# Slot order of the second attention, and identity transposes ahead of three long waits, in a two-layer attention and feed-forward kernel

## The reference, cut to what matters

```python
q, k = rmsnorm(q, q_norm_w), rmsnorm(k, k_norm_w)
scores = einsum('bkgqd,bksd->bkgqs', qg, k) / sqrt(HD)
attn = softmax(scores + where(rel > 0, NEG_INF, slopes * rel))
out = einsum('bkgqs,bksd->bkgqd', attn, v) ... @ Wo.T
w_up = (NF4[codes] * repeat(absmax, 64)).reshape(H, D).T
y2 = relu(x1 @ w_up + b_up + lora) @ w_down + b_down + lora
```

## Time and profile before

| | |
|---|---|
| runs | 1400.67, 1397.17, 1401.01 us; median 1400.67 |
| profiled execution | 1399.04 us; its span 1397.2 us |
| mean granted clock of PE | 0.992 |
| busy | PE 1342.4, DVE 933.1, ACT 880.2, POOL 661.8 us |
| HBM | 61.04 MB moved, mean 44 GB/s |

### The profile page before, as it was taken

One profiled execution on the slowest core, in us unless ns is written; L12 is line 12 of the kernel. 1 busy time (PEld: TensorE's weight loads), 2 busy tenths in 40 slices (PEclk: granted clock), 3 DMA queues, 4 the chain that ended last, 5 costly groups with the idle time before them and its releaser, 6 DMA issues. The chain is left out here.

```text
span 1397.2 us, 21472 instructions
## 1 busy us (share of the span) xinstructions
PE 1342.4 (96%) x7350; PEld 1075.9 (77%) x7350; DVE 933.1 (67%) x1659; ACT 880.2 (63%) x2167; POOL 661.8 (47%) x988
## 2 busy tenths in 40 slices
PE   6899889999999999999999999999999999999997
PEld 5543337888888888888888888888888887778886
DVE  5756655667776776767677767767676767676433
ACT  6246565777676776767777767767677766663211
POOL 5323256555455564535554544645355545443311
PEclk9989999999999999999999999999999999999999
DMA  4100032102010120202020101202020202024010
GB/s 164 53 1 1 0 106 72 31 1 62 26 52 11 52 77 1 62 11 67 2 61 27 52 11 52 72 6 62 3 75 1 62 11 50 9 92 129 27 61 31
DMA packets 36029, 61.04 MB, mean 44 GB/s; under 512 B 9200, under 2 KB 13424, under 8 KB 35920
## 3 DMA queue, kind: packets, MB, share of 16 engines
q1 hardware_dynamic: 35920, 59.66, 13.8%
HBM read 49.68 MB, written 9.96 MB: 43 GB/s over the span
## 5 line engine op out<-in xcount | busy, mean ns | idle before, releaser
L947 POOL TENSOR_TENSOR RI<-SM,C 128x1 f32<-128x1 f32 x256 | 152.2, 595 | 402.7 <-ACT PB L1310 402.4
L1791 DVE TENSOR_TENSOR R<-T,R 128x512 fp32r<-128x512 f32 x288 | 198.8, 691 | 115.2 <-ACT R L1383 104.7
L1784 DVE CUSTOM_DVE_ANT_0 PB<-S,REL,SLC 128x128 f32<-128x128 f32 (+7 forms) x256 | 204.6, 813 | 79.6 <-PE S L2039 76.5
L1310 ACT ACTIVATE PB<-PB,NM 128x128 f32<-128x128 f32 (+7 forms) x256 | 198.2, 774 | 44.7 <-DVE NM L1784 44.1
L1383 ACT ACTIVATE R<-T 128x512 fp32r<-128x512 f32 x288 | 171.4, 595 | 81.2 <-PE T L2428 78.2
L948 POOL TENSOR_SCALAR PB<-PB,RI 128x128 f32<-128x128 f32 (+7 forms) x256 | 209.9, 820 | 25.2
L2428 PE MATMUL T<-C,PB 128*128 128x128 f32 x1152 | 176.0, 276 | 7.7 <-DVE R L1791 3.3
L2428 PEld LDWEIGHTS T<-C,PB 128*128 128x128 f32 x1152 | 135.7, 141 | 37.8 <-DVE R L1791 13.6
L1370 ACT ACTIVATE DQ<-DQ 128x704 f32<-128x704 int32 x128 | 97.5, 785 | 78.6 <-DVE DQ L1865 76.4
L2037 PE MATMUL WB<-R,XT 128*128 128x512 f32 (+1 forms) x268 | 103.9, 388 | 0.0
L2039 PE MATMUL WB<-R,XT 128*128 128x512 f32 (+1 forms) x268 | 103.0, 384 | 0.0
(11 more groups left out here) (311 smaller groups left out, 3502.1 us busy)
## 6 DMA issues: line engine op xcount, KB each, us to landing
RAW<-w SPq DMA_DIRECT2D x85, 256.0 KB, 2.7
DQ<-codes SPq DMA_DIRECT2D x16, 352.0 KB, 4.0
DQ<-absmax SPq DMA_DIRECT2D x16, 352.0 KB, 2.8
dequantised<-DQ SPq DMA_DIRECT2D x16, 352.0 KB, 4.0
PB<-dequantised SPq DMA_DIRECT2D x5, 512.0 KB, 3.7
PB<-x SPq DMA_DIRECT2D x8, 256.0 KB, 4.0
PB<-x_scratch SPq DMA_DIRECT2D x8, 256.0 KB, 3.5
out<-PB SPq DMA_DIRECT2D x8, 256.0 KB, 2.0
```

Of the source, the lines that this page charges most:

```text
L947: ch.link(e.tensor_tensor(RI[:, k:k + 1], SM[:, k:k + 1], C[:, C_EXP + 5:C_EXP + 6], ALU.pow))
L1310: e.activation(pb(m, a, 0, L), pb(m, a, 0, L), ACT.Exp, scale=-1.0, bias=NM[:, k:k + 1], accum_out=SM[:, k:k + 1]).then_inc(exp_done, 1)
L1784: e.tensor_tensor_reduce(out=pb(m, a, 0, L), in0=bank[:, 0:L], in1=REL[:, TOK - L:TOK], scale=SLC[:, a:a + 1], scalar=3.0e38, op0=ALU.add, ...
L1791: e.tensor_tensor(r(o + 512, 512), bank[:, :], rf(o, 512), ALU.subtract).then_inc(t_free, 1)
```

## The change

In `slot_items`:

- `DB` no longer stands beside `DC`. It stays at the front in all slots with a further group and in even slots; in odd slots of the last group it goes behind the first exponential.
- `DC` in slots j = 1 with a further group goes from ahead of the first transpose (`T 0`) to behind it. In slot 57 it goes from the front to behind the last scores.
- `DD` in odd slots of the last group goes behind the third exponential.
- Chunks `W 0` and `W 1` of slot 57 go from between scores and first transpose to behind the first and the second exponential.
- In slot 61 the last exponential and its normalisation (`EX 3`, `NR 3`) go behind `FB 0`.
- `DA` in slots with j % 4 = 1 goes behind the transposes `T 4` to `T 7`; in slots with j % 4 = 3 it stays.

No item that PE takes part in changes its place among PE's own.

In PE's program `keep_warm(bank, n)` issues n transposes of the identity into one 128x128 corner of a bank, with no semaphore: 10 into S[0] ahead of the wait for the fourth Wqk product; 14 into the T bank in `turn_shift(0)`, ahead of the wait for the shifts; and 14 in slot 0's `QK`, behind the ring's wait and ahead of the wait for the scaled queries.

```diff
-    put("DC", "DB", when=0 < n < STEPS - 1 and not (j == 1 and kv))
+    put("DC", when=0 < n < STEPS - 1 and j != 1)
+    put("DB", when=0 < n < STEPS - 1 and (kv or j % 2 == 0))
     ffn(STEPS - 3, ("FB", 1))
     weights("W", 0, 1, when=kv)
     put("PQ", when=s2)
     head(0, "S")
     head(1, "S")
-    put("DC", "DB", when=j == 1 and kv)
     put("DU", when=j == 0)
-    weights("W", 0, 1, when=not kv)
     weights("Q", 0, 1)
     first = j in (1, 7) if kv else j % 2 == 1
     if first:
         keys(0)
+    put("DC", when=j == 1 and kv)
     head(0, "EX")
-    put("DD", when=j % 2 == 1 and n < STEPS - 1)
+    weights("W", 0, when=not kv)
+    put("DB", when=n < STEPS - 1 and not kv and j % 2 == 1)
+    put("DD", when=j % 2 == 1 and kv)
     put("PKV", when=kv)
...
         head(1, "EX", "NR")
+        weights("W", 1, when=not kv)
         head(3, "S")
+        put("DC", when=j == 1 and not kv)
         keys(2)
         ffn(STEPS - 1, ("FV", 1))
         weights("W", 2)
         head(2, "EX", "NR")
+        put("DD", when=not kv and n < STEPS - 1)
         keys(3)
         weights("W", 3)
         weights("Q", 2, 3)
-        head(3, "EX", "NR")
+        if n != STEPS - 3:
+            head(3, "EX", "NR")
         put("QN", when=s2)
         ffn(STEPS - 5, ("FA", 0))
-        ffn(STEPS - 3, ("FB", 0))
+        ffn(STEPS - 3, ("FB", 0), ("EX", 3), ("NR", 3))
         put("WO")
-        put("DA", when=n < STEPS - 1)
+        put("DA", when=n < STEPS - 1 and j % 4 == 3)
         ffn(STEPS - 5, ("FA", 1))
         keys(4, 5, 6, 7)
+        put("DA", when=n < STEPS - 1 and j % 4 == 1)
...
+            def keep_warm(bank, n):
+                for _ in range(n):
+                    e.transpose(bank[:, 0:P], IDENT, IDENT)
...
+            keep_warm(S[0], 10)
             pe.wait_ge(t_free, T_A["QK", 2, 1] + 1)
             qk(*QK_THEN[0])
...
                 mring(k)
+                if u == 0:
+                    keep_warm(T[k % 2], 14)
                 pe.wait_ge(shift_ready, u + 1)
...
                     elif it == "QK":
+                        if known == 0:
+                            ring(at(g, i, "QT"))
+                            keep_warm(T[AT[known, "QT"] % 2], 14)
                         pe.wait_ge(w_free, at(g, i, "PQ") + 1)
```

## The result

The changed kernel takes 1391.36 us in the median of six runs (1388.74 to 1395.60), the kernel before 1400.84 beside it (1396.86 to 1404.00); the ratio is 0.9939 with a 95% interval of 0.9921 to 0.9957. Run again later on another occasion, it gave 1392.48 (1389.79 to 1393.47) against 1400.03, ratio 0.9945 [0.9929, 0.9961]. So some 8 us are gained, against 9.2 forecast.

What follows compares the result with a forecast made beforehand. PE, busy 96% of the span, bounds the kernel; only gaps and low clock can give. 3.6 + 0 + 1.5 + 3.3 = 8.4 off 1399.04 gives 1390.6, said as median 1391.5 us; range 1386.5 to 1398.

Steps and rivals of the forecast that it cites:

- A: Identity transposes do not hold the clock, or the fall only moves elsewhere: median about 1395.5 us; chance 0.28.
- B: Time freed in the attention is met by the next wait and the clock gives little: 1398 us; chance 0.17.
- C: Slower: `DA`'s lines behind the last copies wait for codes or DMA and delay the next scores: 1405.5 us; chance 0.06.
- Part 1: Six slots j = 1 with a further group: `DC` behind the first low half gains 3.6 us, bounds 1.5 to 3.6.
- That is 0.6 each: Gain per slot j = 1 from moving `DC`: 0.44 us of PE idle and the refill behind it, six times.
- Part 2: `DA` behind the last transposes in slots j = 1 and 5: 0.8 of 2.3 us cover used, cost nothing.
- Part 3: Slot 57: reordered copy and chunk halves start the output product 0.7 to 1.5 us earlier; 0.8 taken, bounds -1.0 to 2.4.
- it is wanted at 1163.4: Slot 57: chunk 3's load is issued at 1159.3, about 1 us later than now, but needed only at 1163.4.
- Part 4: Slots 59 and 61: gains of 0.2 us (bounds 0 to 0.6) and 0.5 us (bounds -0.5 to 0.7).
- The last group together: Slots 57, 59 and 61 summed: 1.5 us gained.
- Part 5: Identity transposes hide in PE idles and hold the clock from 66.8 to 77.0 us: 3.3 us gained, 4.6 at most.
- First and third group 0: Transposes at the first and third idles counted as 0, as the clock did not fall there in the profiled execution.

Runs made afterwards that it cites:

- e5: The kernel before with only `DC` moved behind the first transpose in the six slots j = 1 with a further group; 1400.83 us against 1399.00.
- e2: The changed kernel with the old `slot_items` whole and all three groups of identity transposes; 1396.71 us, ratio 0.9987 to the kernel before.
- e3: The changed kernel with the old `slot_items` and only the 14 transposes ahead of the wait for the shifts; 1399.53 us, ratio 0.9998 to the kernel before.
- e1: The changed kernel without any identity transposes, new slot order alone; 1392.75 us, ratio 0.9969 to the kernel before.
- e4: The changed kernel without the 14 transposes ahead of the wait for the shifts; 1394.04 us, ratio 0.9958 to the kernel before.
- e6: The kernel before with only `DA` moved behind the last transposes in all slots with j % 4 = 1; 1395.10 us against 1399.00.
- e8: The changed kernel with 100 identity transposes in place of the 14 in slot 0; 1398.75 us, 10.0 over the changed kernel's profiled execution.

## Why the prediction was right, and where its steps were not

The forecast of 1391.5 stood within 1 us of both medians; the slots and the clock carry the gain, as forecast, and none of the rivals A, B and C decided it. But several of its terms had the wrong reason or size, and their errors partly cancel; that the median fits to 1 us is partly luck.

- **Part 1, 3.6 us.** The size was nearly right, 6 x 0.53 = 3.2, and so was the place, with no wait left where the 0.44 was. But the step "That is 0.6 each" priced `DC` by itself, and by itself it is worth nothing (e5). I named the next late wait as the T2 transpose, 0.25 us away, and of POOL said only that the probabilities are wanted in the next slot. What is late next is the inverse norm in POOL's queue behind the product, then ACT's strict order: rival B's mechanism, on a queue that it did not name. It would have been seen by walking POOL's queue up to its next item that another engine waits for. That the change also held the move that prevents it, priced at 0, is luck of the forecast.
- **Part 2, 0.** It was costed by its cover only, whether it could hurt, and that held: no wait at the slot starts on the low query beyond the cover. That it is the condition for all of part 1, gives up to 0.17 more in a slot j = 5, and takes ACT's waits for the stored block out of these slots, was missed.
- **Part 3, 0.8 for slot 57.** 0.66 measured, but not by the argument made. The output product did start 1.66 us earlier than before (1161.27 with the lead put back), just over the forecast 0.7 to 1.5; but so it does with the old front when the clock doesn't fall. Of the 0.66, 0.5 is the fall that didn't come, 0.5 is `DA`, and the new front lost 0.4 to the late chunk, which the forecast had and called harmless ("it is wanted at 1163.4"). The step that failed is the walk through DVE's work: I compared it with a slot that had run partly at half clock.
- **Part 4.** Slot 59: 0.2, as forecast. Slot 61: 0.8 instead of 0.5, over its bound of 0.7. By PE's rows half of that comes later. The whole idle of 0.94 us ahead of the fourth transpose went, not 0.7 of it, and 0.7 came back as a wait on the low query, which leaves 0.4 at the start of slot 62; there DVE begins with the new scores 0.5 us sooner still, and that is the rest. The first scores of slot 62 on PE, and DVE's first pass over them:

```profile
1227.83 0.50 PE L2044 MATMUL S<-K,R 128*128 128x512 f32 x1 [0.89 <-DVE R L1779]
...
1229.22 0.88 DVE L1791 CUSTOM_DVE_ANT_0 PB<-S,REL,SLC 128x640 f32<-128x640 f32 x1
```

  The wait was 0.18 before. Other traces with the new order in this slot give 0.3 to 1.1, and two with the old one (e2, e3) are 0.4 shorter than the profile of before, so half a microsecond of the gain is scatter of this slot. The last group together, 1.5 forecast, gave 1.8.
- **Part 5, 3.3.** In the pair of profiles it came out almost to the tenth (3.1, value products at 73.50 against 73.3). As a term of the median it was over-sized. A fall at the shift comes in every trace without the group, for 10.2 us in four of them and for 3.4 in three (e1, e4, e6), and keeping the clock there left other idles open. The runs give 2 to 4 us for all groups and none that can be measured for this one alone. "First and third group 0" was wrong for the first, as the fall at 35 in half the traces without it shows; the third has shown no use in any trace.
- **Sum.** Slots 5.7 for 5.1. The two ratios give 8.5 and 7.7 for the whole, so 2.0 to 2.8 are left for the transposes, where 3.3 stood. The pair of profiles lies 10.3 apart because the one after has a single stretch at half clock ahead of its end and the one before has four; that is a draw too.

Rival A had its first half wrong (the transposes do hold the clock) and its second half partly right: a fall that is prevented at one place may come at another.

What stays open: why the clock falls at 85 us in some executions and not in others; why three groups raise the mean clock when the second alone, or the first and third alone, do not; and whether a version with slot 57's old front, which the traces price at some 0.4 us better, would be faster. It wasn't run. None of the kernels run beats the changed one by more than can be measured.

## What to carry to other kernels

Price a moved step by every engine that has a part in it, and follow each queue to the next item that someone waits for: here POOL's share of the step turned 3.2 us into nothing, until a second move took ACT's work out from between. Two moves that are worth nothing and 0.8 us alone can be worth 3.8 together, so measure them together and apart. A stretch at half clock that one profile shows is a draw from several places where it can fall; take its length from several executions, and expect that closing one gap gives little until the others are closed too.

## What the runs showed that I had not expected

- f32 identity transposes keep the granted clock at 1.00 for as long as they run (11.08 us in e8), at 0.111 us each; 14 ahead of a wait took 1.69 us with the fill of the pipe.
- The clock fell in idles of some 2 us: 2.07 to 2.10 at the shift in all seven traces without transposes there.
- The mean granted clock of many plain executions told apart what their times did not: 0.9944 against 0.9917 for e2, whose ratio in time took in no change.
- The same kernel, profiled twice, fell at different places: once at 232.9 alone, then at 84.9, 146.3 and 204.4; the two executions lie 4.6 us apart, nearly half of what the whole change gave.
